# A state-space stage on one core: the convolution's last tap and the skip factor go to ScalarE, softplus runs in two events a batch, and the units of matmuls get a new order over their banks

## The reference, cut to what matters

```python
hs = einsum('blh,dh->bdl', x, W_in_states)        # 1024 channels
gate = einsum('blh,dh->bdl', x, W_in_gates)
conv = sum(conv_w[None, :, j, None] * xpad[:, :, j:j + l] for j in range(4)) + conv_b
hs = silu(conv)                                    # "u" in the kernel
time_step = hs^T W_dt^T;  dt = softplus(time_step @ W_dtproj.T + b_dtproj)
Bm, Cm = hs^T W_b^T, hs^T W_c^T                    # 16 states
dA = exp(A * dt);  dBu = dt * Bm * hs
s = dA * s + dBu   (over the 256 positions);  y = einsum('lbdn,bln->bdl', h, Cm)
y = (y + hs * D) * silu(gate);  out = einsum('bdl,od->blo', y, W_out)
```

## Time and profile before

| what | value |
|---|---|
| median of three executions | 3369.53 us (3364.22 to 3376.11) |
| the profiled execution, its own time | 3367.53 us |
| its span, first to last instruction | 3365.7 us |
| busy over the span | PE 91%, DVE 83%, ACT 72%, POOL 62% |
| first scan of batch 0, of batch 1 | 52.85 us, 171.58 us |
| first scan of batch 8, of batch 9 | 940.34 us, 1050.07 us |
| first scan of batch 15 | 1711.77 us |

### The profile page before, as it was taken

The page is one execution under the profiler, slowest core; times in us unless marked ns, Lnnn a source line. Parts: engine busy times, 40 slices in busy tenths (PEclk is TensorE's granted clock), DMA queues, the critical chain, the costliest instruction groups (busy, mean ns, idle before and its releaser), DMA issues. The chain is left out here.

```text
span 3365.7 us, 46151 instructions
## 1 busy us (share of the span) xinstructions
PE 3051.1 (91%) x16134; PEld 1828.5 (54%) x16134; DVE 2789.0 (83%) x2773; ACT 2407.5 (72%) x4531; POOL 2093.1 (62%) x1207
## 2 busy tenths in 40 slices
PE   7899999999999999999985799899999999879998
PEld 5677667766776667666754334344343433234444
DVE  6999999999999998999997777677777777378886
ACT  4877788778787877778774267566666666657776
POOL 5999989999999999999987134333433433200000
PEclk9999999999999999999997799999999999989999
DMA  4012210222022202221123545554555464131111
GB/s 166 31 43 76 76 56 30 76 76 79 8 79 76 76 13 73 76 76 32 55 91 99 162 140 154 166 171 146 169 172 168 138 182 143 46 116 45 45 45 35
DMA packets 164376, 311.86 MB, mean 93 GB/s; under 512 B 22736, under 2 KB 80208, under 8 KB 164000
## 3 DMA queue, kind: packets, MB, share of 16 engines
q1 hardware_dynamic: 158784, 299.53, 27.9%
q10 hardware_dynamic: 5360, 9.38, 1.1%
HBM read 217.16 MB, written 91.69 MB: 92 GB/s over the span
## 5 line engine op out<-in xcount | busy, mean ns | idle before, releaser
L820 POOL TENSOR_TENSOR bu<-du,bc 128x1024 f32<-128x1024 f32 x512 | 1196.7, 2362 | 82.6 <-DMA bc<-bc_scratch 70.8
L698 ACT ACTIVATE states<-dt,negA 128x256 f32<-128x256 f32 x2048 | 852.2, 463 | 359.7 <-DVE hc L917 334.5
L904 DVE TENSOR_TENSOR_SCAN states<-states,bu 128x1024 f32<-128x1024 f32 x352 | 805.9, 2289 | 73.8 <-ACT states L698 69.1
L1556 DVE TENSOR_REDUCE mmax<-s_ps 128x2 f32<-128x1024 f32 x512 | 624.5, 1224 | 256.0 <-PE s_ps L1275 239.7
L1400 ACT ACTIVATE pt<-s_ps 128x512 f32<-128x512 f32 x1024 | 572.9, 596 | 339.7 <-PE s_ps L1284 330.7
L917 DVE TENSOR_TENSOR hc<-states,bc 128x1024 f32<-128x1024 f32 x352 | 430.8, 1224 | 41.1 <-DVE states L904 6.4
L518 PE MATMUL y_ps<-id_sb,hc 128*128 128x128 f32 x2816 | 380.2, 279 | 83.7 <-DVE hc L917 83.7
L518 PEld LDWEIGHTS y_ps<-id_sb,hc 128*128 128x128 f32 x2816 | 323.9, 143 | 209.6 <-DVE hc L917 171.0
L1284 PE MATMUL s_ps<-qst,kst 105*128 105x512 bf16 x1024 | 381.2, 388 | 11.7 <-ACT pt L1400 5.1
L829 POOL TENSOR_TENSOR hp<-hp,bc 128x1024 f32<-128x1024 f32 x160 | 377.6, 2360 | 16.3 <-DVE hp L904 16.0
L1275 PE MATMUL s_ps<-kst,qst 102*128 102x512 bf16 x1024 | 320.9, 396 | 57.2 <-DMA kst<-mask_d 46.7
(11 more groups left out here) (172 smaller groups left out, 4247.0 us busy)
## 6 DMA issues: line engine op xcount, KB each, us to landing
bc<-bc_scratch SPq DMA_DIRECT2D x128, 512.0 KB, 7.8
stack_d<-parts SPq DMA_DIRECT2D x180, 256.0 KB, 3.0
qst<-stack_d SPq DMA_DIRECT2D x64, 384.0 KB
kst<-stack_d SPq DMA_DIRECT2D x64, 384.0 KB
x<-xres SPq DMA_DIRECT2D x31, 512.0 KB, 4.9
w_raw<-in_w_ffn SPq DMA_DIRECT2D x48, 256.0 KB, 2.7
w_raw<-in_w_ffn SPq DMA_DIRECT2D x16, 768.0 KB, 7.3
xT_sb<-in_xT SPq DMA_DIRECT2D x16, 512.0 KB, 3.3
```

Of the source, the lines that this page charges most:

```text
L698: a = act.activation(states[:, bank, first:first + SEQ], dt[:, t, :], ACT.Exp, scale=negA[:, t, c * NS + n:c * NS + n + 1])
L820: pool.tensor_tensor(bu[:, buf, :].rearrange("p (n l) -> p n l", n=NS), du[:, t % (2 * GRP):t % (2 * GRP) + 1, :].to_broadcast([P, NS, SEQ ...
L904: m = dve.tensor_tensor_scan(dst, src, bu[:, BU_OF[k][0], half * 2 * SEQ:(half + n) * 2 * SEQ], 0.0, ALU.mult, ALU.add)
L1556: dve.tensor_reduce(mmax[:, u // HG, c:c + 2], s1_ps[:, pair], AX.X, ALU.max).then_inc(s1_free, 1)
```

## The change

1. Convolution: `c` units have three matmuls instead of four, 8 fewer a batch. When ScalarE evacuates an `s` unit it also writes, in place in PSUM, the last tap's product plus the bias; the three matmuls add to that.
2. Skip term: ScalarE writes u * D to a new tile `ud` (`scale_skip`, once a channel tile, two steps ahead), and TensorE adds it with two transposes in place of two fp32 matmuls.
3. Softplus: `d` units 2 and 3 are evacuated together and so are 0 and 1: one table load in and one out for four activations. The last two units are now made in the batch before (0 and 1) or in step 1 (2 and 3), and `weigh_inputs` has steps of its own (`WEIGH_AT`).
4. Units have a new order and a bank each by a table (`BANK_OF`).

```diff
-PRODUCTS = {"s": HK, "c": TAPS, "g": HK, "l": 2 * DT, "d": GRP, "t": GRP * SEQT, "o": DT}
+PRODUCTS = {"s": HK, "c": TAPS - 1, "g": HK, "l": 2 * DT, "d": GRP, "t": GRP * SEQT, "o": DT}
...
-SHORT = [(0, "d", 1, 0), (3, "t", 3, -1), (6, "d", 2, 0), (11, "t", 0, 0), (12, "d", 3, 0), (18, "t", 1, 0),
-         (23, "d", 0, 1), (26, "t", 2, 0)]
+SHORT = [(1, "d", 2, 0), (1, "d", 3, 0), (3, "t", 3, -1), (11, "t", 0, 0), (17, "t", 1, 0),
+         (24, "d", 0, 1), (24, "d", 1, 1), (26, "t", 2, 0)]
...
-SKIP_COST = 0.5
+SKIP_COST = 0.3
...
-SOFT = 2
+WEIGH_AT = (28, 1, 9, 17)
...
+UD_LEAD = 2
...
-                        m = pe.matmul(proj[:, 0:SEQ], diagW[:, i, k, :], xpad[:, i % 2, k:k + SEQ], start=start, stop=stop)
+                        m = pe.matmul(proj[:, 0:SEQ], diagW[:, i, k, :], xpad[:, i % 2, k:k + SEQ], start=False, stop=stop,
+                                      skip_group_check=True)
...
-                    pe.matmul(y_ps[:, i, :], u[:, par, t, i * P:(i + 1) * P], diagD[:, t, :],
-                              start=(i == 0), stop=False, skip_group_check=True)
+                    m = pe.matmul(y_ps[:, i, :], ud[:, t % 2, i * P:(i + 1) * P], id_sb[:, :], start=(i == 0), stop=False,
+                                  is_transpose=True, skip_group_check=True)
...
-                    act.activation(xpad[:, i % 2, TAPS - 1:], proj[:, 0:SEQ], ACT.Copy).then_inc(ev["s"], 1)
+                    a = act.activation(xpad[:, i % 2, TAPS - 1:], proj[:, 0:SEQ], ACT.Copy)
+                    if f > 0:
+                        a = act.activation(proj[:, 0:SEQ], proj[:, 0:SEQ], ACT.Identity,
+                                           bias=chan_sb[:, i, C_CONVB:C_CONVB + 1],
+                                           scale=chan_sb[:, i, C_TAP + TAPS - 1:C_TAP + TAPS])
+                    a.then_inc(ev["s"], 1)
...
-                    act.preload_act_table_set("softplus")
+                    if i % 2 == 0:
+                        act.preload_act_table_set("softplus")
...
-                    act.preload_act_table_set("exp_and_others")
+                    if i % 2 == 1:
+                        act.preload_act_table_set("exp_and_others")
+
+            def scale_skip(b, par, t):
+
+                if t == 0:
+                    act.wait_ge(u_ready, b + 1)
+                if b * DT + t > 1:
+                    act.wait_ge(skip_mm, b * DT + t - 1)
+                act.activation(ud[:, t % 2, :], u[:, par, t, :], ACT.Copy, scale=chan_sb[:, t, C_D:C_D + 1]).then_inc(ud_ready, 1)
...
+                    t = (k + UD_LEAD) // CPT
+                    if (k + UD_LEAD) % CPT == 0 and active(b + t // DT):
+                        scale_skip(b + t // DT, par if t < DT else 1 - par, t % DT)
```

More of the change, by code:

```diff
@@ L196, in state_space_phase @@
                    for i, kind in enumerate("kq")}
-        a_small = [own_d[:, 6 * HID + 4 * i:6 * HID + 4 * i + SEQT] for i in range(6)]
-        a_qkb = own_d[:, 6 * HID + 24:6 * HID + 28].rearrange("p (o i) -> p o i", o=2)
+        a_small = [a_sm[:, 4 * i:4 * i + SEQT] for i in range(6)]
+        a_qkb = a_sm[:, 24:28].rearrange("p (o i) -> p o i", o=2)
         a_sum, a_mean, a_sq, a_ve, a_half, a_rs = a_small
@@ L303, in unit_before @@
         def unit_before(pos, b, front=False):
[L305 to L308, removed]
-                    return kind, seq(kind, b + off, i)
[L310 to L315, removed]
+            if front:
+                if pos < PROJ:
+                    return None
+                kind, i, off = FRONT[pos - PROJ]
+                return kind, seq(kind, b + off, i)
+            bank = BANK_OF[UNITS[pos][:2]]
+            for kind, i, off in UNITS[pos - 1::-1] if pos else ():
+                if BANK_OF[kind, i] == bank and active(b + off):
+                    return kind, seq(kind, b + off, i)
+            if b == 0:
+                last = [(x, q % PROJ) for q, x in enumerate(FRONT)]
+            else:
+                last = [(x, BANK_OF[x[:2]]) for x in UNITS]
+            for (kind, i, off), at in last[::-1]:
+                if at == bank and active(b - 1 + off):
                     return kind, seq(kind, b - 1 + off, i)
@@ L497, in unit, with skip_term @@
                     m.then_inc(mm[kind], 1)
-            def skip_term(b, par, t):
-                if not (isinstance(b, int) and b == 0 and t == 0):
+            def skip_term(b, t):
+                pe.wait_ge(ud_ready, b * DT + t + 1)
+                if b * DT + t > 0:
                     pe.wait_ge(y_ready, b * DT + t)
                 for i in range(SEQT):
-                    pe.matmul(y_ps[:, i, :], u[:, par, t, i * P:(i + 1) * P], diagD[:, t, :],
-                              start=(i == 0), stop=False, skip_group_check=True)
+                    m = pe.matmul(y_ps[:, i, :], ud[:, t % 2, i * P:(i + 1) * P], id_sb[:, :], start=(i == 0), stop=False,
+                                  is_transpose=True, skip_group_check=True)
+                m.then_inc(skip_mm, 1)
             def sum_states(b, k):
@@ L606, in body @@
                                 pe.wait_ge(ev[kind0], value)
-                            unit(pos % PROJ, kind, i, b + off, par if off == 0 else 1 - par, lo, hi)
+                            unit(BANK_OF[kind, i], kind, i, b + off, par if off == 0 else 1 - par, lo, hi)
                     if k % CPT == 0:
-                        skip_term(b, par, k // CPT)
+                        skip_term(b, k // CPT)
                     if k not in POOL_STEPS:
@@ L655, in evacuate @@
                         act.wait_ge(ev["c"], i - 1)
[L656 removed]
+                    a = act.activation(xpad[:, i % 2, TAPS - 1:], proj[:, 0:SEQ], ACT.Copy)
[4 more added lines that the diff above has]
+                    a.then_inc(ev["s"], 1)
                 elif kind == "c":
[L658 to L659 removed]
+                    act.activation(u[:, par, i, :], proj[:, 0:SEQ], ACT.Copy).then_inc(ev["c"], 1)
                 elif kind == "g":
@@ L760, in front @@
                         silu_tile(i - 1)
+                scale_skip(0, 0, 0)
             def body(b, par):
@@ L851, in body @@
                     for j in range(GROUPS):
-                        for start in when(b, k, SP_AT[j] + SOFT):
-                            if active(start + (j in AHEAD)):
-                                weigh_inputs(pool, start + (j in AHEAD), par if (start is b) == (j not in AHEAD) else 1 - par, j)
+                        if k == WEIGH_AT[j] and j == 0 and active(b + 1):
+                            weigh_inputs(pool, b + 1, 1 - par, 0)
+                        elif k == WEIGH_AT[j] and j:
+                            weigh_inputs(pool, b, par, j)
                     if k == W_AT[-1] + 2:
@@ L869, in _ @@
             for t in range(DT):
-                for j in range(TAPS):
+                for j in range(TAPS - 1):
                     dve.tensor_scalar(diagW[:, t, j, :], id_sb[:, :], chan_sb[:, t, j:j + 1], None, ALU.mult)
-                dve.tensor_scalar(diagD[:, t, :], id_sb[:, :], chan_sb[:, t, C_D:C_D + 1], None, ALU.mult)
             dve.drain()
@@ L891, in front @@
                 dve.engine_nop().then_inc(mm["c"], PER["c"])
-                for j in AHEAD:
-                    weigh_inputs(dve, 0, 0, j)
+                weigh_inputs(dve, 0, 0, 0)
             def scan(b, k):
```

25 lines of the change are left out of this document (16 added, 9 removed).

## The result

The changed kernel takes 3400.76 us (median of four, 3396.59 to 3407.92), the one before beside it 3371.07 (3364.22 to 3376.11): 1.0092 times as long, 95% interval 1.0065 to 1.0118. It is 0.9% slower, and within 3 us of the forecast's 3398. Its profiled run, the slowest of the four, spans 3406.0 us, against 3365.7.

The account below looks back on a forecast made before the run. VectorE sets the batch; its stops grow from 5.92 to 8.20 us, +2.28 a batch. 31.9 (14 batches) + 1.9 (batch 0) + 1.5 (last batch) - 5 (before first scan) = +30.3: 3367.53 becomes 3398 us, range 3367 to 3418.

Parts of the forecast that it names:

- the clock: Rival, chance 0.02: TensorE at 1.2 GHz for a quarter of the time, 9 us a batch left, 3525 us.
- 4, scan behind softplus 2 and 3: VectorE before scan 4: decays wait behind a softplus event of 4.30 us; new stop 0.72 us.
- 4, tile product, TensorE late by its banks: VectorE at step 4's finished tile: TensorE waits for bank evacuations behind step 4's decays; stop about 0.95 us, 1.27 before.
- 15, 26: VectorE's stops at these steps: their softplus events are gone, so -1.18 and -0.89 us.
- 18 (SiLU on u): VectorE before scan 18: SiLU moves behind step 17's decays, a narrower window; stop 2.41 us in place of 1.00.
- 21: VectorE's stop at step 21, behind its own scan with no named cause: 0.46 us, kept unchanged.
- 27 (softplus 0 and 1): VectorE before scan 27: softplus event in step 26 plus one `ud`; stop 2.12 us in place of 0.89.
- 31: VectorE before scan 31: SiLU on the gates stays and one `ud` follows it; 1.12 us becomes 1.54.
- the front: Before the first scan: VectorE builds 16 of 40 diagonals less, -6.8 us, 1.4 taken back; -5 us taken.
- GpSimd setting the pace: Rival, chance 0.09: GpSimd's shorter waits shorten a batch by 3.1 us; 48 us faster in all, 3319 us.
- The no-change case: Rival, chance 0.09: evacuations don't reach TensorE, `ud` hides, step 21's stop moves off; +0.03 us a batch, 3367 us.
- TensorE late at 8, 12 and 16: Rival, chance 0.16: `c` units 3 and 5 wait in their banks, TensorE 0.6 us late at two steps; +18 us, 3416.

Follow-up runs that it names:

- The fillers: Changed kernel plus useless identity matmuls into an unread part of `y_ps`, eight ahead of `s` unit 1, twelve ahead of step 27's sums: 3385.76 us, ratio 1.0062.
- the order alone: Changed kernel with the old four taps and the skip by diag(D), keeping new order, banks and paired softplus: 3385.8 us, ratio 1.0052 to the kernel before.

## Why the prediction was right

The sign was right, and so was the mechanism: VectorE sets the batch, and the change merges and moves table events into windows where scans wait longer. That the time came within 3 us was luck, since two errors cancel: the stops were forecast 0.98 us a batch too long (13.7 us in 14 batches), and the clock, which the sum left out, cost 19.2 us, 15.2 more than in the kernel before. With the clock whole in both kernels the stage would have grown by some 15 us, half of the forecast (my estimate: 30.5 - 15.2). By its own steps:

| step | forecast | measured, full clock | with lower clock |
|---|---|---|---|
| 4, scan behind softplus 2 and 3 | 0.72 | 0.54 | 0.54 |
| 4, tile product, TensorE late by its banks | 0.95 (its own terms give 0.99) | 0.90 | 2.07 |
| 15, 26 | gone | gone | gone |
| 18 (SiLU on u) | 2.41 | 2.24 | 2.25 |
| 21 | 0.46 kept | gone | gone |
| 27 (softplus 0 and 1) | 2.12 | 2.02 | 2.02 |
| 28, tile product | none | none | 1.28 |
| 31 | 1.54 | 1.53 | 0.62 |
| sum | 8.20 | 7.23 | 8.78 |
| batch | 112.0 | 111.03 | 112.67 |

- **A batch.** Forecast +2.28; measured +1.30 at full clock. The difference is mostly step 21's stop, which I kept and which went (0.46), and a softplus event of 4.17 for 4.30, counted twice. The step that was mis-sized is the clock: 0.02 chance of a large loss, nothing in the main sum. It costs 1.6 to 1.7 us in ten of the batches 1 to 14 and 2.84 in batch 3, 19.2 us in all over 14 batches of 111.03. The fillers show it as the cause: they leave the order of units and all of ScalarE's work as they are, and take it away.
- **Sum over the stage.** Batches 1 to 14 grew by 33.4 (1573.6 for 1540.2; forecast 31.9), the front lost 4.2 (forecast 5), batch 0 went from 118.73 to 115.53, -3.2 where I had +1.9: it had stops of 1.50 before scan 3, 3.44 at step 4's tile and 1.09 at step 28's, which went, and got one of 1.94 before scan 4; I had not looked at them. The last batch cost +4.5, where my estimate was +1.5, with a stop of 2.02 at step 3. To the last scan that makes -4.2 - 3.2 + 33.4 + 4.5 = +30.5 (1856.34 for 1825.82), forecast +30.3. The stages behind it are untouched; they took 1540 us before, 1550 in the change's profiled run and 1536 to 1553 in all these runs, which follows no edit.
- **Prices.** `ud` 0.50 and the tap 0.52 as single events, for 0.42; but the stops grew by 0.4 for each `ud` (e.g. 1.12 to 1.53), since records overlap at their ends (`ud` at 1012.57, next decays at 1012.96). Softplus, four in 1.57, for 1.74.
- **TensorE.** Busy 97.98, forecast some 95. The convolution is down 3.8 (forecast 4.0); the skip is 4.9 to 3.1 us, 1.8 for 2.8: two transposes take 0.38, not 0.26. None of it shows in the time, as foreseen.
- **Table loads.** The event's loads take 1.28, and the next activation starts 1.29 after each, so 5.1 us of loads were saved and not 10.6. The Trainium skill (ScalarE: Activation LUTs, What ACT_TABLE_LOAD costs) adds a drain of about 1.4 us to each; no row here has room for one.
- **Rivals.** GpSimd setting the pace: its softplus wait went, its wait for B rows is 3.8 to 4.6 (3.2 before), and one short stop of VectorE in batch 8 names `bu`, where batches 7 and 9 have the same 0.62 and name the decays. The no-change case: needed `ud` to hide, and it doesn't, where it stands behind a long event. TensorE late at 8, 12 and 16: no such stop. Late at one place more it is, at step 28, but by its clock. The clock: right in kind, a seventh in size (19 us, where that case had 127 over the forecast). The Trainium skill's rule that transposes don't count as work for the clock (TensorE: Matmul & The Clock Gate, Part 4: PE-mode transpose) is not settled here: 288 of the 512 records of batch 2 are transposes and its clock is 1.00; the idle stretch at step 27 is followed by transposes alone, the one near step 4 by matmuls first, and matmuls put in front held the clock at both. Fillers that are transposes weren't tried. But the added transposes are not needed: with the order alone, where the skip is matmuls, batch 2 took 111.45 at 0.98 and batch 3 110.80 at 1.00.

Open: why step 21's product starts 0.46 late behind its own scan in the two kernels that have diag(D) and four taps in the order of before or of after, and in no other; and why batches 2 and 5 keep the clock over the same idle stretches (1.90 and 2.84 us in batch 2) after at least one of which each of the others loses it.

## What to carry to other kernels

Where decays or other short work chain two engines, a long event on the side engine costs what its window lacks, and merging two events saves their loads only where a load was on the path: compare each event with the window in which it stands, not its engine's total. One number for a whole kind of unit (a lag, a lead) hides opposite needs; with the lag set by unit and `ud` by tile, the same change went from 30 us slower to 17 us faster than before. Table the stops of the engine that sets the pace, by step: they add, and each run then tells which edit to keep.

## What the runs showed that I had not expected

- TensorE's clock fell after idle stretches of 1.9 and 2.8 us inside a batch in which TensorE is busy 89% of the time (mean granted clock 0.79 over 958:966, 0.83 over 1040:1050), and eight transposes then took 1.91 to 1.97 us for 1.04 to 1.09. Those are the times at the lower level, 1.2 GHz (0.50 in the row 961.70:963.40), where the full one is 2.4.
- Work that nobody reads made the kernel faster: with 20 more matmuls a batch (TensorE 102.4 us busy for 98.0) batch 15 starts 17.7 us sooner, and the profiled span is 3392.8 for 3406.0. It pays only in idle: where the wait was gone, the same eight brought a stop of 0.20 us a batch.
- The kernel before has such batches too: 5 and 10 to 12 take 110.36 to 111.72, and of batch 11 the windows view says

```profile
1270.17:1381.89 111.72, 104.90 (x544) 77.92 (x544) 101.66 (x65) 87.42 (x182) 103.00 (x52) 0.97 0.18 59
```
